# A gathered per-sample matmul with a residual: every turn as block diagonals, and loads split around the gather

## The reference

```python
def _L0_cond_ref(x, conditions, weights):
    w = weights[conditions]
    return jnp.einsum('bct,bcd->bdt', x, w)
x = x + _L0_cond_ref(x, itok_B_1_198, L0_cond_weights)
```

## Time and profile before

| | us |
|---|---|
| median of 3 runs | 47.14 |
| lowest, highest | 46.56, 47.2 |
| the profiled execution, whole | 46.28 |
| its span, first to last instruction | 45.0 |

### The profile page before, as it was taken

The page is one execution under the profiler, slowest core; times in us unless marked ns, Lnnn a source line. Parts: engine busy times, 40 slices in busy tenths (PEclk is TensorE's granted clock), DMA queues, the critical chain, the costliest instruction groups (busy, mean ns, idle before and its releaser), DMA issues.

```text
span 45.0 us, 294 instructions
## 1 busy us (share of the span) xinstructions
PE 23.1 (51%) x98; PEld 9.9 (22%) x98; DVE 14.9 (33%) x24; ACT 13.9 (31%) x16; POOL 1.6 (4%) x9
## 2 busy tenths in 40 slices
PE   0040000000000079999999999999999999200000
PEld 0040000000000034243463453443544433000000
DVE  1310000000019940069999900820720753600000
ACT  0899100000000050068988800800710733500000
POOL 4009000000000000000000000000000000000000
PEclk9999999999999999999999999999999999999955
DMA  0679999999999999999999999999999999999993
GB/s 0 124 299 423 423 423 430 430 423 437 423 423 430 430 423 437 423 423 430 408 437 423 423 437 423 415 444 415 423 437 415 430 430 423 423 430 426 383 415 146
DMA packets 2594, 17.83 MB, mean 396 GB/s; under 512 B 290, under 2 KB 290, under 8 KB 546
## 3 DMA queue, kind: packets, MB, share of 16 engines
q1 hardware_dynamic: 2448, 16.78, 89.9%
q0 software_dynamic: 144, 1.05, 5.5%
q10 hardware_dynamic: 2, 0.00, 0.0%
HBM read 9.44 MB, written 8.39 MB: 396 GB/s over the span
## 4 chain that ended last, share of the span: by engine, by line
PE 51%; DMA 24%; DVE 8%; issue 2%; DVEq 0%
PE product L143 31%; DMA gathered<-weights,table_row 22%; PE product L147 19%; DVE w_all L173 5%; DMA condition<-conditions 3%; DVE y_sb L186 2%; PE product L130 1%; DVE row_along L161 1%; DVE gathered L170 1%; DVE table_row L164 0%; DVEq L167 0%
## 5 line engine op out<-in xcount | busy, mean ns | idle before, releaser
L147 PE MATMUL product<-x_sb,w_all 64*64 64x512 f32 x64 | 8.6, 696 | 13.0 <-DVE w_all L173 13.0
L143 PE MATMUL product<-x_sb,w_diag 128*128 128x512 f32 x32 | 14.0, 595 | 0.0
L182 DVE COPY y_sb<-product 128x1024 f32<-128x1024 f32 x7 | 8.6, 1224 | 10.2 <-PE product L143 6.8
L111 ACT COPY y_sb<-product 128x1024 f32<-128x1024 f32 x7 | 7.1, 1012 | 10.9 <-PE product L143 7.4
L143 PEld LDWEIGHTS product<-x_sb,w_diag 128*128 128x128 f32 x32 | 6.0, 190 | 7.9 <-issue 7.9
L147 PEld LDWEIGHTS product<-x_sb,w_all 64*64 64x64 f32 x64 | 3.4, 206 | 17.5 <-DVE w_all L173 13.1
L107 ACT COPY w_diag<-w_all 64x256 f32<-64x256 f32 x4 | 2.6, 639 | 11.3 <-DVE w_all L173 11.3
L170 DVE TENSOR_TENSOR gathered<-gathered,piece 128x64 f32<-128x64 f32 x1 | 0.3, 268 | 10.2 <-DMA gathered<-weights,table_row 10.2
L173 DVE STREAM_TRANSPOSE w_all<-gathered 128x2048 f32<-128x2048 f32 x1 | 2.3, 2312 | 0.0
L102 ACT COPY w_diag<-zero 64x1024 f32<-64x1024 f32 x2 | 2.1, 1042 | 0.0
L186 DVE COPY y_sb<-product 128x512 f32<-128x512 f32 x2 | 1.4, 691 | 1.5 <-PE product L143 1.5
(11 more groups left out here) (5 smaller groups left out, 0.5 us busy)
## 6 DMA issues: line engine op xcount, KB each, us to landing
x_sb<-x SPq DMA_DIRECT2D x8, 1024.0 KB, 14.2
out<-y_sb SPq DMA_DIRECT2D x7, 1024.0 KB, 7.0
out<-y_sb SPq DMA_DIRECT2D x2, 512.0 KB, 5.8
condition<-conditions ACTq DMA_DIRECT2D x1, 0.2 KB
gathered<-weights,table_row POOLq DMA_INDIRECT x1, 9.8
```

The source lines that it names most:

```text
L111: nc.scalar.copy(y_sb[:, 4 * turn:4 * turn + 2, :], product[turn % SETS][0][:, :, :]).then_inc(moved_by_act, 1)
L143: product_of = nc.tensor.matmul(product[turn % SETS][j][:, g, :], w_diag[:, n - 4 * TILED, :], x_sb[:, n, :], start=True, stop=True)
L147: product_of = nc.tensor.matmul(product[turn % SETS][h][halves(g), j, :], w_all[halves(h), :, n], x_sb[halves(h), n, :], start=True, stop= ...
L182: nc.vector.tensor_copy(y_sb[:, 4 * turn + 2:4 * turn + 4, :], product[turn % SETS][1][:, :, :]).then_inc(moved_by_dve, 1)
```

## The change

`TILED` goes: all 32 pairs are multiplied as block diagonals, and `w_diag` holds all 32 pairs. ACT and DVE fill the blocks of turns 0 and 1 before the first move and those of turn n + 2 ahead of the moves of turn n; PE waits for the blocks of turns 0 and 1 by two new semaphores (for later turns its wait for the moves of turn n - 2 covers them). SP issues the load of turn 0 and of the first pair of turn 1 (pair 4, `BRIDGE`), waits until that pair has landed, and only then issues the other three pairs of turn 1 (`BEHIND`) and the six other loads. PE, once pair 4 has landed, makes three products of it with itself into a PSUM bank that nobody reads before it is written again. With the small product that spreads the rows this makes 1 + 3 + 32 = 36 matmul calls. PE's wait for `one` is dropped. The output has one layout for all pairs, which changes how the host reads it, not the stores' shapes.

```diff
-    TILED = TURNS // 2
+    BRIDGE, BEHIND = slice(4, 5), slice(5, 8)
...
-        w_diag = sbuf("w_diag", [P, PAIRS - 4 * TILED, PAIR * D], fp32)
+        w_diag = sbuf("w_diag", [P, PAIRS, PAIR * D], fp32)
...
         def on_sync(sp):
-            for turn in range(TURNS):
+            sp.dma_start(x_sb[:, pairs_of(0), :], x[:, pairs_of(0), :]).then_inc(x_loaded[0], 16)
+            sp.dma_start(x_sb[:, BRIDGE, :], x[:, BRIDGE, :]).then_inc(x_loaded[1], 16)
+            sp.wait_ge(x_loaded[1], 16)
+            sp.dma_start(x_sb[:, BEHIND, :], x[:, BEHIND, :]).then_inc(x_loaded[1], 16)
+            for turn in range(2, TURNS):
                 sp.dma_start(x_sb[:, pairs_of(turn), :], x[:, pairs_of(turn), :]).then_inc(x_loaded[turn], 16)
...
-                               zero[halves(h), :].unsqueeze(2).to_broadcast([C, PAIRS - 4 * TILED, D]))
+                               zero[halves(h), :].unsqueeze(2).to_broadcast([C, PAIRS, D]))
             act.wait_ge(w_ready, 1)
-            for turn in range(TURNS):
-                if turn < TILED:
-                    nc.scalar.copy(w_diag[halves(0), pairs_of(turn), 0:D],
-                                   w_all[halves(0), :, pairs_of(TILED + turn)].rearrange("p d n -> p n d"))
-                if turn < LAST:
+            for turn in range(-SETS, LAST):
+                if turn + SETS < TURNS:
+                    nc.scalar.copy(w_diag[halves(0), pairs_of(turn + SETS), 0:D],
+                                   w_all[halves(0), :, pairs_of(turn + SETS)].rearrange("p d n -> p n d")
+                                   ).then_inc(w_placed_by_act, 1)
+                if turn >= 0:
                     act.wait_ge(multiplied, turn + 1)
...
-            pe.wait_ge(one_set, 1)
...
-            pe.wait_ge(w_ready, 1)
+            pe.wait_ge(x_loaded[1], 16)
+            for _ in range(3):
+                nc.tensor.matmul(product[1][1][:, 1, :], x_sb[:, BRIDGE.start, 0:P], x_sb[:, BRIDGE.start, :],
+                                 start=True, stop=True)
             for turn in range(TURNS):
-                pe.wait_ge(x_loaded[turn], 16)
-                if turn >= SETS:
+                pe.wait_ge(x_loaded[turn], 32 if turn == 1 else 16)
+                if turn < SETS:
+                    pe.wait_ge(w_placed_by_act, turn + 1)
+                    pe.wait_ge(w_placed_by_dve, turn + 1)
+                else:
                     pe.wait_ge(moved_by_act, turn - SETS + 1)
                     pe.wait_ge(moved_by_dve, turn - SETS + 1)
...
-                        if turn >= TILED:
-                            product_of = nc.tensor.matmul(product[turn % SETS][j][:, g, :], w_diag[:, n - 4 * TILED, :],
-                                                          x_sb[:, n, :], start=True, stop=True)
-                            continue
-                        for h in range(PAIR):
-                            product_of = nc.tensor.matmul(product[turn % SETS][h][halves(g), j, :],
-                                                          w_all[halves(h), :, n], x_sb[halves(h), n, :],
-                                                          start=True, stop=True)
+                        product_of = nc.tensor.matmul(product[turn % SETS][j][:, g, :], w_diag[:, n, :], x_sb[:, n, :],
+                                                      start=True, stop=True)
...
-            for turn in range(LAST):
-                if turn < TILED:
-                    nc.vector.tensor_copy(w_diag[halves(1), pairs_of(turn), D:PAIR * D],
-                                          w_all[halves(1), :, pairs_of(TILED + turn)].rearrange("p d n -> p n d"))
-                dve.wait_ge(multiplied, turn + 1)
+            for turn in range(-SETS, LAST):
+                if turn + SETS < TURNS:
+                    nc.vector.tensor_copy(w_diag[halves(1), pairs_of(turn + SETS), D:PAIR * D],
+                                          w_all[halves(1), :, pairs_of(turn + SETS)].rearrange("p d n -> p n d")
+                                          ).then_inc(w_placed_by_dve, 1)
+                if turn >= 0:
+                    dve.wait_ge(multiplied, turn + 1)
```

More of the change, by code:

```diff
@@ L51, in conditioned_residual_kernel @@
         w_all = sbuf("w_all", [P, D, PAIRS], fp32)
-        w_diag = sbuf("w_diag", [P, PAIRS - 4 * TILED, PAIR * D], fp32)
-        product = [[ctx.enter_context(nc.psum_tensor(f"product{s}_{h}", [P, 2, T], fp32)) for h in range(PAIR)]
+        w_diag = sbuf("w_diag", [P, PAIRS, PAIR * D], fp32)
+        product = [[ctx.enter_context(nc.psum_tensor(f"product{s}_{j}", [P, 2, T], fp32)) for j in range(2)]
                    for s in range(SETS)]
@@ L59, in conditioned_residual_kernel @@
         condition_loaded = semaphore("condition_loaded")
-        one_set = semaphore("one_set")
         zero_set = semaphore("zero_set")
@@ L68, in conditioned_residual_kernel @@
         w_ready = semaphore("w_ready")
+        w_placed_by_act = semaphore("w_placed_by_act")
+        w_placed_by_dve = semaphore("w_placed_by_dve")
         multiplied = semaphore("multiplied")
@@ L154, in on_vector @@
             nc.vector.memset(zero[:, :], 0.0).then_inc(zero_set, 1)
-            nc.vector.memset(one[:, :], 1.0).then_inc(one_set, 1)
+            nc.vector.memset(one[:, :], 1.0)
             for q in range(P // Q):
@@ L176, in on_vector @@
             dve.wait_ge(w_ready, 1)
-            for turn in range(LAST):
-                if turn < TILED:
-                    nc.vector.tensor_copy(w_diag[halves(1), pairs_of(turn), D:PAIR * D],
-                                          w_all[halves(1), :, pairs_of(TILED + turn)].rearrange("p d n -> p n d"))
-                dve.wait_ge(multiplied, turn + 1)
-                nc.vector.tensor_copy(y_sb[:, 4 * turn + 2:4 * turn + 4, :], product[turn % SETS][1][:, :, :]
-                                      ).then_inc(moved_by_dve, 1)
+            for turn in range(-SETS, LAST):
[5 more added lines that the diff above has]
+                    dve.wait_ge(multiplied, turn + 1)
+                    nc.vector.tensor_copy(y_sb[:, 4 * turn + 2:4 * turn + 4, :], product[turn % SETS][1][:, :, :]
+                                          ).then_inc(moved_by_dve, 1)
             for j in range(2):
@@ L218 @@
     laid = np.asarray(result.results[0]["out"])
-    tiled = laid[:, :B // 4].reshape(2, D, B // 16, PAIR, 2, T).transpose(2, 4, 0, 3, 1, 5).reshape(B // 2, D, T)
-    whole = laid[:, B // 4:].reshape(PAIR, D, B // 4, T).transpose(2, 0, 1, 3).reshape(B // 2, D, T)
-    return np.concatenate([tiled, whole])
+    return laid.reshape(PAIR, D, B // PAIR, T).transpose(2, 0, 1, 3).reshape(B, D, T)
```

## The result

The changed kernel takes 47.8 us (median of 6 runs, 47.4 to 48.6) against 47.16 of the kernel before (46.2 to 47.21). The ratio is 1.028 with a 95% interval of 1.016 to 1.040; it uses only the runs within 1.5% of each kernel's fastest (five after, two before), which is why it is larger than the ratio of the two medians. The profiled execution has a span of 46.2 us and 47.5 in all, 1.2 us above the profiled one of before in both. The forecast was 47.3 with a range of 46.5 to 49.0 and "no change" as the likeliest case. The time lies in the range, but the change is a small loss (whether of more than 2% the interval leaves open), and its size is that of a term that I had put at 0.1 us.

A forecast was written before the change was run, and what follows sets the result against it. The prediction took the DMA transfers (17.83 MB at 426 GB/s) as the bound. A 0.1 us hole and PE 0.1 late, not added twice but allowing for rounding, made span 45.0 + 0.2; median 47.14 + 0.2 = 47.3 us, range 46.5 to 49.0.

The forecast's parts named there:

- The floor is the transfers, and no order can win: DMA engines: 17.83 MB at 426 GB/s take 41.9 us of the 45.0 span; no order wins more than about a microsecond.
- The time, 47.3 us: Whole kernel: span 45.0 + 0.2 = 45.2; by difference from the median of the runs, 47.14 + 0.2 = 47.3, no change.
- The gather was late because loads stood ahead of it, not by a latency of its own: Gather's start: most of its 3.1 us without bytes is queueing; first byte now at 5.7, landed at 9.5.
- Rival one: Gather's start: the 7.6 us first byte is POOL's latency, PE starts at 15.9; span 48.1, 50.2 us; chance 0.12.
- rival two: Gather shares with the pair from 5.0, the pair is told at 8.7, a 1.6 us hole opens; 48.7 us; chance 0.13.
- PE's chain and slack: PE: 3.4 us from landing to first product, eight turns 27.7 us, start needed by 12.8, forecast 12.9, 0.1 late.
- The three products hold the clock: PE before turn 0: unread products end between 8.8 and 11.3, rest only 1.6 to 4 us, turn 0 at full level.
- rival three: PE's turn 0 starts at the low clock level and costs 1.8 us more; 49.0 us; chance 0.10.
- The hole in the transfers: DMA engines between the pair's last bytes (5.6) and the gather's first (5.7): idle for 0.1 us.
- the sign that I had named for it: DMA share: near 1.00 from 2.75 to 44 if right; an empty stretch between 5.6 and 10 if wrong.

The follow-up runs named there:

- the run that waits for the issue: Changed kernel, but SP waits until POOL has issued the gather instead of for the pair to land; 47.09 us, ratio 1.007.
- The run that started at 13.23: Changed kernel with two pairs instead of one ahead of the gather and SP waiting for the gather's issue; 46.72 us, ratio 1.010.
- the sibling above: Changed kernel with two pairs ahead of the gather as two loads, SP waiting for the first pair's landing; median 46.92 us, ratio 1.007.
- wait for load 0: Changed kernel, but SP waits for the load of turn 0 to land instead of for the pair; ratio 1.034, span 46.6 us.

## Why the prediction was right or wrong

- *The floor is the transfers, and no order can win:* right of the span. No version's span is shorter than that of the kernel before (45.0), and the spans of all that were not held up by PE follow the loads within 0.2 us. It is not right of the metric, since the medians of some versions lie lower by the time around the span, of which the prediction says nothing.
- *The time, 47.3 us:* in part luck. The forecast of the span, 45.2, was a microsecond too low (46.2 in the profiled execution). But the forecast also added 0.86 us, by which the profiled execution of before lay below its median. It has the size of the longer time around the span, and the changed kernel's six runs do not have that: 46.5, the middle of their spans, and 1.3 give the 47.8. The two misses point opposite ways and leave 0.5.
- *The gather was late because loads stood ahead of it, not by a latency of its own:* right. Its first packets came at 5.3 (5.7 forecast), 0.9 us after POOL's issue had ended (4.43), and it landed by 9.1 (9.5). Rival one is out; so is rival two, since the pair landed by 6.28, and the gather came in only as its last packets moved. The rule of the Trainium skill that was set beside rival two ("DMA: Bandwidth & Descriptors", section Queues, rings and completion order: engines take turns between queues, packet by packet) did not show between the gather and the loads issued just behind it, if a packet is what the trace counts as one: in the run that waits for the issue the gather's packets went first (88.5% against 0.5% from 5.7 to 8), and the measurement decides.
- *PE's chain and slack:* right. 3.4 us from landing to the first product, 27.7 for eight turns, and a limit near 12.8 for the start. The run that started at 13.23 was 0.2 to 0.3 late by it, with turn 6's store at its bare 4.0 us.
- *The three products hold the clock:* turn 0 ran at the full pace here, so the outcome is right; the reason given for it is not. I had taken the one rest of 4.3 us, after which the level fell in the kernel before, as the rest that PE may have. In the thirteen traces the level fell between 2.0 and 5.4 us after PE's last product, and in the sibling above after a rest of 2.1 us, which lies within the 1.6 to 4 us that I allowed. The rest was 1.3 us here, shorter than any that I had allowed, so the outcome is in part luck. A turn 0 at the low level cost 2.8 us in two traces and 1.7 in a third (6.5 and 5.4 against 3.7), where rival three has 1.8.
- *The hole in the transfers:* wrong, and this is the step that failed: "Then the hole is 0.1 us." I counted when the queue would be empty and took full rate from the first byte. No engine stood empty, but the gather's first packets, with little else under way, came at 334 GB/s from 5.25 to 7.25 (0.43 us), SP's loads behind it came slowly too when they were issued after it had begun (404 GB/s from 8.50 to 11.00, 338 to 381 in siblings), and these loads were uneven, so that the last of the sixteen steps of turn 6's load fell 0.5 us further behind the middle one than before. In sum 1.2 us where 0.1 stood. The kernel's own start should have told me: the earlier trace rows show 213 GB/s in the first microsecond of a stream. And the sign that I had named for it could not show it: the DMA share stayed near 1.00, as I had asked of a right forecast.
- *The chances:* the case that came is none of the rivals. It is the forecast's own term, mis-sized by a microsecond, which moves it from no change to a loss at about the edge of what can be told.

What stays open: why a stream's first packets are slow, and why loads issued after the gather has begun come slowly and unevenly. Waiting for the landing instead of the issue causes the second (the pairs of runs with one and with two pairs ahead agree), and a shorter wait by 0.7 us did not cure it. The steps of turn 6's load show it more clearly than the rates do: they spread over 0.6 us before, over 0.7 to 1.5 in the five kernels that issue the loads while the gather moves, over 0.45 where they are issued after its landing, over 0.3 to 0.4 in four of the five that issue them ahead of its first packets, and over 0.9 in the fifth, where the gather itself was uneven. The mechanism wasn't found.

## What to carry to other kernels

Where the DMA engines are the floor, as here, moving one transfer ahead of others won nothing in the span by itself, and a change of stream that wasn't covered by queued work was paid at the end in full. If a transfer has to go first, let the queue behind it be filled when it is issued, not when something has landed, and put enough ahead of it to cover its own start: with both done (two pairs, wait for the issue) 0.9 us of the 1.2 came back, and most of the rest was PE's. Count the bytes of a stretch, not its busy share: the share was 1.01 while a fifth of the bandwidth was missing. And before a forecast goes from a profiled execution to a median, split the time of several runs into the span and what lies around it: a change need not carry the second part over.

## What was not expected of the hardware

The DMA engines' busy share stays at 1 while packets of a fresh stream take longer: 334 GB/s at a share of 1.01, against 426 at the same share. A gather was served ahead of loads issued just behind it, while in the kernel before it shared evenly with loads issued before it. The granted clock fell after 2.1 us of rest in one execution and held over 1.3 us in another; after the last product of a kernel it fell 2.0 us later at the earliest (two pairs, wait for the issue) and 5.4 at the latest (wait for load 0). And a granted clock of 1.00 in the profile can stand where the trace holds no entry for it.
